# A graph kernel's third layer: features stored beside exponents, added to the gathered rows ahead of the product

## The reference

```
def _L2_gnn_ref(node_h, edge_h, src, dst, W_fc, W_fcr, loop_W):
    h = node_h @ W_fc.T
    eh = edge_h @ W_fcr.T
    alpha = _segment_softmax(eh, dst, N)
    z = h[src]
    agg = jax.ops.segment_sum(alpha * (z + eh), dst, num_segments=N)
    ...
    h_new = jnp.where((deg > 0)[:, None], agg + h @ loop_W, h)
    return jax.nn.relu(h_new)
...
    h = jnp.maximum(_layernorm(x, axis=-1), 0.0)
    x = x + _L2_gnn_ref(h, edge_attr_64, src, dst, L2_gnn_W_fc, L2_gnn_W_fcr, L2_gnn_loop_W)
```

## Time and profile before

| | |
|---|---|
| time, median of 3 runs | 6794.79 us (6792.39 to 6797.38) |
| time of the profiled execution | 6794.83 us |
| its span in the trace | 6792.9 us |
| PE busy | 5199.7 us (77%) |
| DVE busy | 4658.1 us (69%) |
| ACT busy | 3734.0 us (55%) |
| POOL busy | 3315.8 us (49%) |
| third layer's visits on PE (L1773) | 941.8 us busy |
| third layer's gathers on POOL (L1154) | 1611.7 us busy |

### The profile page before, as it was taken

How to read it: one execution, slowest core, us unless ns; L and a number is a source line. 1 busy time by engine, 2 the same in 40 slices (tenths; PEclk the granted TensorE clock), 3 DMA queues, 4 the chain that set the end, 5 groups by cost and what they waited for, 6 DMA issues and landing times.

```text
span 6792.9 us, 129349 instructions
## 1 busy us (share of the span) xinstructions
PE 5199.7 (77%) x47386; PEld 4664.9 (69%) x47387; DVE 4658.1 (69%) x6434; ACT 3734.0 (55%) x3046; POOL 3315.8 (49%) x3412
## 2 busy tenths in 40 slices
PE   0046558888888726999999999756888888788886
PEld 0012137777777726999999999755777777777776
DVE  9846558888888767888887888634555555555554
ACT  0101137777777625887777787401555455454565
POOL 0467777777777721000000000277777777777730
PEclk9988779999999968999999999877999999899998
DMA  9988987777777636666676666434777777676785
GB/s 350 353 244 262 285 281 237 238 232 239 241 239 235 186 95 170 193 198 193 193 195 181 194 200 195 134 82 107 157 153 160 152 154 151 144 157 147 159 140 112
DMA packets 1691090, 1314.15 MB, mean 193 GB/s; under 512 B 920211, under 2 KB 1555092, under 8 KB 1690032
## 3 DMA queue, kind: packets, MB, share of 16 engines
q1 hardware_dynamic: 872085, 948.47, 47.3%
q10 hardware_dynamic: 705808, 299.82, 18.6%
q0 software_dynamic: 112592, 57.76, 5.2%
HBM read 833.36 MB, written 311.54 MB: 169 GB/s over the span
## 4 chain that ended last, share of the span: by engine, by line
PE 41%; DVE 7%; ACT 5%; issue 4%; DMA 3%; POOL 3%; DVEq 1%; SPq 0%; ACTq 0%; POOLq 0%
PE pair L1653 22%; PE pair L1773 8%; PE wide L1797 6%; ACT u L1547 3%; POOL u L1154 3%; ACT batch L1547 1%; DMA extra<-hi_b,tsel 1%; PE wide L1836 1%; DMA u<-zrows,stage 1%; DVE u L921 1%; DMA u<-cells 1%; DVEq L417 1%; DVE batch L986 1%; DVE u L618 0%; ACT u L1404 0%
## 5 line engine op out<-in xcount | busy, mean ns | idle before, releaser
L1653 PE MATMUL pair<-tab,u 128*128 128x192 bf16 (+1 forms) x29106 | 2537.7, 247 | 186.7 <-ACT u L1404 181.1
L1653 PEld LDWEIGHTS pair<-tab,u 128*128 128x128 bf16 x29106 | 2467.5, 98 | 208.4 <-ACT u L1404 184.1
L1404 ACT ACTIVATE u<-u 128x1792 bf16<-128x1792 uint8 (+1 forms) x1360 | 2272.3, 1701 | 434.6 <-PE pair L1653 211.9
L1154 POOL DMA_INDIRECT u<-zrows,stage x1664 | 1611.7, 969 | 1315.7 <-DMA zrows<-batch 783.2
L1119 POOL DMA_INDIRECT cells<-val,idx x1664 | 1614.0, 970 | 754.4 <-issue 490.7
L618 DVE TENSOR_REDUCE u<-u 128x1792 bf16<-128x1792 uint8 (+1 forms) x838 | 1673.7, 2020 | 396.0 <-PE pair L1653 258.5
L1773 PE MATMUL pair<-u 128*128 x4880 | 941.8, 351 | 399.0 <-DVE u L921 380.7
L1773 PEld LDWEIGHTS pair<-u 128*128 128x128 f32 x4880 | 858.4, 204 | 474.7 <-issue 473.2
L1547 ACT ACTIVATE u<-u 128x1792 bf16<-128x1792 uint8 x317 | 524.7, 1684 | 309.6 <-PE wide L1797 303.0
L1613 PE MATMUL wide<-u,wbd 128*128 128x512 f32 x840 | 511.1, 700 | 193.1 <-DMA u<-in_ea 97.6
L1797 PE MATMUL wide<-u 128*128 128x193 bf16 x5544 | 521.5, 246 | 36.3 <-ACT u L1547 30.0
(11 more groups left out here) (270 smaller groups left out, 4374.7 us busy)
## 6 DMA issues: line engine op xcount, KB each, us to landing
u<-cells SPq DMA_DIRECT2D x2100, 224.0 KB, 3.1
cells<-zt SPq DMA_DIRECT2D x100, 1568.0 KB, 15.7
u<-in_ea SPq DMA_DIRECT2D x420, 256.0 KB
ex_d<-u ACTq DMA_DIRECT2D x420, 256.0 KB
u<-ex_d SPq DMA_DIRECT2D x208, 512.0 KB
u<-gate_d SPq DMA_DIRECT2D x420, 64.1 KB
u<-gate_d ACTq DMA_DIRECT2D x420, 64.0 KB
cells<-val,idx POOLq DMA_INDIRECT x1664
```

The source lines that it names most:

```text
L1154: pool.indirect_dma_start(out=ring3[:, slot, k, :], out_offset=None, in_=zrows, in_offset=bass.IndirectOffsetOnAxis(ap=stage[:, st, c:c + ...
L1404: return S.activation(to, of, ACT.Copy)
L1653: mm = M(acc(p, t // 2 * 2 + b)[:, 0:width], ring[:, q % nr, (b * CK + k) * P:(b * CK + k + 1) * P], table[:, j, 0:width], start=j == 0 an ...
```

## The change

The row of an edge in `ex_d` becomes [ex | eh] in place of [ex | eh * ex]. In the backward step the product `bwd_mul` on DVE goes; ACT copies `eh` out of PSUM instead (`kept`), right behind its exponential, and PE waits for both before it transposes. In the third layer `product` becomes two DVE operations: first z + eh into the third part of the `exr` row, which also frees the gather's slot, then, after a wait for that result, ex * (z + eh) into the second part. PE waits for the second (a new semaphore, `more`). The product's moving operand is then the first 128 columns, and so are the closing product and the copy of the sums; the batch chain loses the step that added the two numerators.

```diff
-            def bwd_mul(st):
-                dve.wait_ge(b_ex, st + 1)
-                if st:
-                    dve.wait_ge(b_full, st * NB)
-                V.tensor_tensor(xe, eh[st % 2], b_pm[st % 3], ALU.mult).then_inc(b_xe, 1)
...
             def product(g):
                 dve.wait_ge(s3["rows_ready"], g + 1)
-                V.tensor_tensor(exr[:, ds(g % XR, 1), :, 2 * F:F3].rearrange("p o k c -> p (o k) c"),
-                                exr[:, ds(g % XR, 1), :, 0:F].rearrange("p o k c -> p (o k) c"),
-                                ring3[:, ds(g % SLOTS, 1), :, :].rearrange("p o k c -> p (o k) c"),
-                                ALU.mult).then_inc(s3["slots_free"], 1)
+                ex, e, both = [exr[:, ds(g % XR, 1), :, a * F:(a + 1) * F].rearrange("p o k c -> p (o k) c") for a in range(3)]
+                V.tensor_tensor(both, e, ring3[:, ds(g % SLOTS, 1), :, :].rearrange("p o k c -> p (o k) c"),
+                                ALU.add).then_inc(s3["slots_free"], 1)
+                dve.wait_ge(s3["slots_free"], g + 1)
+                settle(dve)
+                V.tensor_tensor(e, ex, both, ALU.mult).then_inc(s3["more"], 1)
...
-                        V.tensor_copy(agg[:, a7, :], bank[a % 2][:, 0:F3]).then_inc(s3["sums_used"], 1)
+                        V.tensor_copy(agg[:, a7, 0:2 * F], bank[a % 2][:, 0:2 * F]).then_inc(s3["sums_used"], 1)
...
-                            chain(s3, base, 3, V.tensor_tensor(cen[:, :, :], agg[:, :, F:2 * F], agg[:, :, 2 * F:F3], ALU.add))
-                            chain(s3, base, 4, V.tensor_tensor(sq[:, :, :], cen[:, :, :], hrow[:, :, :], ALU.mult))
...
+                            chain(s3, base, 3, V.tensor_tensor(sq[:, :, :], agg[:, :, F:2 * F], hrow[:, :, :], ALU.mult))
...
+            def kept(st):
+                if st:
+                    act.wait_ge(b_full, st * NB)
+                S.activation(xe, eh[st % 2], ACT.Copy).then_inc(b_xe, 1)
...
                 if "C" in part and k < STEPS:
                     exps(k)
+                    kept(k)
...
                 if j == 0:
+                    pe.wait_ge(b_ex, st + 1)
                     pe.wait_ge(b_xe, st + 1)
...
                 def visit(g, v, first):
-                    pe.wait_ge(s3["slots_free"], g + 1)
+                    pe.wait_ge(s3["more"], g + 1)
...
-                        mm = M(bank[a % 2][:, 0:F3], ohf[not first][:, k, :], exr[:, ds(g % XR, 1), k, :].rearrange("p o c -> p (o c)"),
+                        mm = M(bank[a % 2][:, 0:2 * F], ohf[not first][:, k, :], exr[:, ds(g % XR, 1), k, 0:2 * F].rearrange("p o c -> p (o c)"),
                                start=first and k == 0, stop=False)
...
-                M(bank[a % 2][:, 0:F3], zb[:, 0:P], zb[:, 0:F3], start=False, stop=True).then_inc(s3["sums_ready"], 1)
+                M(bank[a % 2][:, 0:2 * F], zb[:, 0:P], zb[:, 0:2 * F], start=False, stop=True).then_inc(s3["sums_ready"], 1)
```

More of the change, by code:

```diff
@@ L293, in gnn_kernel @@
         exl = [sem(f"exl{i}") for i in range(XR)]
-        s3 = {n: sem(f"{n}_3") for n in ("rows_ready slots_free oh_ready oh_free sums_ready sums_used step var root "
+        s3 = {n: sem(f"{n}_3") for n in ("rows_ready slots_free more oh_ready oh_free sums_ready sums_used step var root "
                                          "ex_free more_ready more_free").split()}
@@ L300, in gnn_kernel @@
         NB = BL // 2
-        N3 = 15
+        N3 = 14
         ORD = {0: 0, 1: 0, 2: 1}
@@ L806, in _ @@
                         bwd_before(k + 1)
-                    if "D" in part:
-                        bwd_mul(k)
             for n in (T - 2, T - 1):
@@ L986, in _ @@
                             chain(s3, base, 2, V.reciprocal(hrow[:, :, :], sq[:, :, :]))
[L987 to L989 removed]
+                            chain(s3, base, 3, V.tensor_tensor(sq[:, :, :], agg[:, :, F:2 * F], hrow[:, :, :], ALU.mult))
+                            chain(s3, base, 4, V.tensor_tensor(cen[:, :, :], sq[:, :, :], seven(hk, m), ALU.add))
                             settle(dve)
[L991 removed]
+                            chain(s3, base, 5, V.scalar_tensor_tensor(seven(xs, m), cen[:, :, :], 0.0, seven(xs, m), ALU.max, ALU.add))
                             settle(dve)
[L993 removed]
+                            chain(s3, base, 6, V.tensor_reduce(mean7[:, :], seven(xs, m), AX.X, ALU.add))
                             settle(dve)
[L995 removed]
+                            chain(s3, base, 7, V.scalar_tensor_tensor(cen[:, :, :], each(mean7[:, :]), -1.0 / F, seven(xs, m),
                                                                       ALU.mult, ALU.add))
[L997 removed]
+                            chain(s3, base, 8, V.tensor_tensor(sq[:, :, :], cen[:, :, :], cen[:, :, :], ALU.mult))
                             settle(dve)
@@ L1001, in _ @@
                             settle(dve)
-                            chain(s3, base, 10, V.reciprocal(rs7[:, :], sd7[:, :]))
+                            chain(s3, base, 9, V.reciprocal(rs7[:, :], sd7[:, :]))
                             settle(dve)
-                            chain(s3, base, 11, V.scalar_tensor_tensor(hrow[:, :, :], cen[:, :, :], 0.0, each(rs7[:, :]), ALU.max, ALU.mult))
+                            chain(s3, base, 10, V.scalar_tensor_tensor(hrow[:, :, :], cen[:, :, :], 0.0, each(rs7[:, :]), ALU.max, ALU.mult))
                             settle(dve)
-                            chain(s3, base, 12, V.tensor_copy(seven(tab[0], m), hrow[:, :, :]))
-                            chain(s3, base, 13, V.tensor_tensor(cen[:, :, :], hrow[:, :, :], seven(tab[0], m), ALU.subtract))
+                            chain(s3, base, 11, V.tensor_copy(seven(tab[0], m), hrow[:, :, :]))
+                            chain(s3, base, 12, V.tensor_tensor(cen[:, :, :], hrow[:, :, :], seven(tab[0], m), ALU.subtract))
                             settle(dve)
-                            chain(s3, base, 14, V.tensor_copy(seven(tab[0], m, F, 2 * F), cen[:, :, :]))
-                            chain(s3, base, 15, V.tensor_tensor(seven(tab[0], m, 2 * F, F3), cen[:, :, :],
+                            chain(s3, base, 13, V.tensor_copy(seven(tab[0], m, F, 2 * F), cen[:, :, :]))
+                            chain(s3, base, 14, V.tensor_tensor(seven(tab[0], m, 2 * F, F3), cen[:, :, :],
                                                                 seven(tab[0], m, F, 2 * F), ALU.subtract))
```

## The result

The changed kernel takes 6899.73 us (median of 4 runs, 6895.62 to 6903.93) where the kernel before takes 6793.59 (6788.46 to 6797.38): 1.0157 of its time, 95% interval 1.0139 to 1.0174. Forecast were 6889 us; the medians are 106 us apart where the sum said 94. The profiled execution has a span of 6901.8 us, 108.9 more than before.

A forecast was written before the change was run, and what follows sets the result against it. The prediction took the scatter to end the edge pass and a loop over PE, SP and DVE to space third-layer visits; 84.6 - 8.5 + 18 = +94 us on 6794.8 gave 6889 us, range 6815 to 6985.

The forecast's parts named there:

- The loop: Third layer, turns 1 to 6: PE, SP and DVE in a loop space new chunks, 2.94 us before, 3.8 after.
- X: Third layer: delay of every new chunk by the second DVE operation, 0.93 us, between 0.66 and 1.17.
- +84.6 for the regular tiles: Turns 1 to 6: 72 tiles with no batch chain ahead lose 1.06 us with two new chunks, 1.89 with three.
- +18 for the clock: Turns 1 to 6: PE's longer pauses lower its clock, 0.25 us per tile, 72 times; bounds 0 and 108 us.
- -8.5 for the batch chain: Batch chain: one step fewer, 0.65 us with its gap, gained 13 times while PE waits for it.
- about 1/10: Regular tiles: share of last visits expected to run at a slow clock, costing some 1.5 us each.
- The rival in which every tile starts cold: Turns 1 to 6: last visit and what follows start cold each time, +108 in place of 18 us, 6979 us; chance 0.1.
- The tiles behind a batch chain: Turns 1 to 6, 12 tiles: PE's saving and DVE's addition roughly cancel, 0, between -0.8 and +1.1 us each.
- The term of 0: Backward steps: ACT's added copies cost nothing, hidden behind the scatter with 89.9 us of slack; at worst +34 us.
- The rival in which ACT sets the edge pass: Backward steps: all 124 us of ACT's copies lengthen them, +34 us on top, 6923 us; chance 0.06.
- The columns don't decide: Against the rival that PE bounds third-layer visits, which then shrink until POOL sets the pace: 6764 us, chance 0.1.
- Absorbed: Rival, turns 1 to 6: the slower chain uses up SP's 37.5 us of gather waits, no change, 6792 us; chance 0.08.

The follow-up runs named there:

- e4: The changed kernel with 14 products of zeros on PE ahead of each visit to a new chunk: 6891.34 us, 1.0138 of the kernel before.
- e2: The changed kernel with the third layer's products, closing product and copy over 192 columns again: 6958.43 us, 1.0238 of the kernel before.
- e1: The changed kernel without the multiplication by ex, so one DVE operation per chunk and 128 columns: 6764.95 us, 0.9955 of the kernel before.
- e8: The kernel before with SP handing over chunks as soon as landed and DVE forming its product one chunk ahead: 6765.09 us, 0.9960 of the kernel before.
- e3: The kernel before with only the change's backward steps, third layer untouched: 6809.38 us, 1.0020 of the kernel before.
- e9: The kernel before with only the change's backward steps, plus 410 semaphore instructions in DVE's steps: 6795.87 us, 1.0001 of the kernel before.
- e10: The changed kernel with 410 semaphore instructions added to DVE's backward steps: 6894.67 us, 1.0142 of the kernel before.

## Why the prediction was right, and where its sum was off

*The loop.* X was put at 0.93 us and is 0.94 (0.69 and 0.25); the visits at 3.8 us apart and are 3.78; the first visit's weight loads at 1.87 and are 1.86; the copies at 21.3 and 25.4 us and are 21.15 and 25.69 in the tiles shown. The pause behind the wait and the register instruction was read from two steps of the batch chain, a place that has nothing to do with the change but the same instructions. The Trainium skill's rule that was set against it ("VectorE: DVE Perf Modes", "The DRAIN you can't avoid"), by which the sum would be 40 us smaller, is not what the run shows for this pair: 51.8 us of waiting ahead of 208 second operations. The batch chain of the kernel before separates the parts, in the median of its steps: behind a wait alone a step starts 0.03 us after its predecessor's end (L1007; so far the rule agrees), with the semaphore instruction `settle` in between 0.15 us (L1004), and with a register instruction besides 0.24 (L1006). So the pause comes from the two instructions that stand between, of which the prediction named only one.

*The sum over the turns.* +84.6 for the regular tiles, +18 for the clock and -8.5 for the batch chain were to make 94; turns 1 to 6 grew by 110.6 us. The regular tiles grew by 124.0, of which e4 and e2 give the clock about 28 to 31 us, not 18, so **the clock is the term that was too small**. The visits of the 72 regular tiles, counted in the timeline of the weight loads, show which part of it. Of the second visits that have another behind them, 36 of 71 take over 2.0 us, near the 5/9 taken from the edge pass, and the loop does hide them: the next visits are 5 us late in all (0.30 at 5224.34), where 8 were set. But 17 of the 72 last visits are slow, where "about 1/10" would be 7, and they cost 27 us in place of 11. **The share of slow last visits is what was mis-sized.** In tiles with two new chunks (the 40 with early sums and not next to a chain tile), the mean length is 21.37 us without a slow visit, 21.39 with only the second slow, and 23.11 with the last one slow. Turn 2's clock came out at 0.91, inside the 0.85 to 0.94 that I had named. The rival in which every tile starts cold, +108 us, was further off. With 5 + 27 = 32 us for the clock, some 7 of the 124.0 are left over; the long pauses of the place of DVE's code, which was in no term, would be about that, but in this kernel that is not shown.

*The tiles behind a batch chain.* I set 0 and -8.5 for the shorter chain, and got -13.3. By e2 that is two errors that partly cancel, which was luck: the second operation costs these 12 tiles 3.5 + 7.8 = 11 us, if the shorter chain is worth its 0.65 us in each, and the columns give back 16.8.

*The edge pass.* The term of 0 held, the sign behind it did not: I expected the steps to become slower by a part of ACT's 124 us, with SP's wait shorter than 89.9 us. ACT had idle time enough, and what PE had waited for was DVE's multiplication; the steps' own work became 95 us shorter and SP waits 184.6 us. That the scatter hides them either way is what made the 0 safe. The rival in which ACT sets the edge pass fell.

*The other rivals.* The columns don't decide, as the loop of 3.78 us shows; but the 6764 us that this rival named is a real floor, to which e1 and e8 came. Absorbed, it was not: the waits for gathers of 37.5 us did vanish, and the loop ate far more.

*Open:* the stretch from the last copy to the end took 265.0 us before, 262.2 after, 267.3 in e4 and 273.7 in e3, in code that is the same. With e9 it was 265.2 and with e10 267.1, so the place of DVE's code alone doesn't order these, and one execution each may be too few; I have not followed it.

## What to carry to other kernels

Work that moves from PE to another engine was dear here because that engine did it on the loop that spaces PE's work: follow the loop from one visit to the next in a timeline and count what the moved operation adds there, its wait included. Before shortening an engine's work, ask whether it is waited for; here a reordering of SP's queue took 97 us off the changed kernel, and the 64 columns fewer 59 (e2). And what a change frees in a stage that another transfer hides (95 us here) is not a gain until that transfer is shorter.

## What was not expected of the hardware

The place of a loop's code in DVE's instruction stream has a price: with 410 instructions taken out 2000 us earlier, the pause ahead of a tile's first product was about 1.49 us in place of 1.10 in the same four tiles of five turns, and the kernel 13 us slower (1.0020, 1.0010 to 1.0029); with 410 idle instructions put in, 1.0001 (0.9992 to 1.0010). The Trainium skill, "Runtime: NRT & Kernel Launch", section "Instruction fetch mechanics", says that instructions are brought in block by block in sequence, and that a branch to a target outside the blocks held has to wait for a fetch. That place matters would agree with it, but no row here ties a fetch to these pauses.

The price of a column depends on the clock that the work before it has left: the same 64 columns saved 31 us in 72 tiles where PE's growing pauses lowered the clock (59 by the arithmetic at full clock), and 16.8 us in the 12 tiles behind a batch chain, in each of which one visit ran at a low clock in both kernels (3.49 us with 128 columns, 4.16 to 4.98 with 192).
